# An expert stage that goes by experts in place of tiles of 128 tokens, with routing masks in bf16

## The reference, cut to what matters

```python
x = x + tanh(g_xattn[0]) * attention(layernorm(x), ctx, Wq, bq, Wk, bk, Wv, bv)   # B=8, S=256, H=256, 120 keys
h = layernorm(x)                                     # 2048 tokens of 256
logits = einsum('sbh,eh->sbe', h, router_w)          # E=8 experts
routing = argmax(logits, axis=-1)                    # one expert for each token
for e in range(8):
    mask = (routing == e)[..., None]
    xe = where(mask, h, 0.0)
    g = einsum('sbh,ih->sbi', xe, gate_w[e])         # I=704
    u = einsum('sbh,ih->sbi', xe, up_w[e])
    out = out + where(mask, einsum('sbi,hi->sbh', silu(g) * u, down_w[e]), 0.0)
x = x + tanh(g_ffn[0]) * out
```

## Time and profile before

| what | value |
|---|---|
| median of 3 runs | 226.1 us (225.43 to 228.0) |
| span of the profiled execution, first to last instruction | 218.9 us |
| median less span, what lies around the span | 7.2 us |
| TensorE, share of the span busy | 91% (199.7 us) |
| VectorE, ScalarE, GpSimd | 60%, 50%, 62% |
| granted TensorE clock, mean over the span | 0.960 |

### The profile page before, as it was taken

The page is one execution under the profiler, slowest core; times in us unless marked ns, Lnnn a source line. Parts: engine busy times, 40 slices in busy tenths (PEclk is TensorE's granted clock), DMA queues, the critical chain, the costliest instruction groups (busy, mean ns, idle before and its releaser), DMA issues.

```text
span 218.9 us, 4538 instructions
## 1 busy us (share of the span) xinstructions
PE 199.7 (91%) x1200; PEld 170.9 (78%) x1200; DVE 130.8 (60%) x430; ACT 109.8 (50%) x223; POOL 136.1 (62%) x138
## 2 busy tenths in 40 slices
PE   7899999997665789999999999999999999999960
PEld 3667998985564678888888888888888888888850
DVE  2886899867699125537555537564636565645650
ACT  1478777664500534495269485369475444422410
POOL 3004099495473897339966998987998985212111
PEclk9999999999787589999999999999999999999996
DMA  6999315928600319621581085194003012011000
GB/s 208 340 394 378 135 49 163 368 73 291 217 0 0 99 25 358 211 68 38 189 313 32 0 311 189 34 383 126 1 8 92 0 51 68 9 49 51 5 28 20
DMA packets 11845, 29.43 MB, mean 134 GB/s; under 512 B 1986, under 2 KB 8517, under 8 KB 10790
## 3 DMA queue, kind: packets, MB, share of 16 engines
q1 hardware_dynamic: 6320, 20.20, 25.9%
q0 software_dynamic: 2064, 5.12, 7.8%
q10 hardware_dynamic: 3430, 3.74, 5.1%
HBM read 24.85 MB, written 4.72 MB: 135 GB/s over the span
## 4 chain that ended last, share of the span: by engine, by line
PE 83%; DVE 6%; ACT 3%; DMA 3%; issue 2%; ACTq 1%; POOL 0%; POOLq 0%; DVEq 0%
PE ps L929 36%; PE ps L941 12%; PE ps L908 6%; PE ps L944 5%; PE ps L790 3%; PE ps L729 3%; PE ps L770 3%; DMA both<-in_ctxT 3%; PE ps L811 3%; PE ps L759 2%; PE ps L901 2%; PE ps L800 2%; PE ps L750 2%; PE ps L878 1%; DVE V L1193 1%
## 5 line engine op out<-in xcount | busy, mean ns | idle before, releaser
L929 PE MATMUL ps<-wgu,xhT 128*128 x360 | 83.1, 384 | 1.2 <-DVE xhT L1229 1.2
L929 PEld LDWEIGHTS ps<-wgu,xhT 128*128 128x128 f32 x360 | 66.3, 191 | 12.5 <-issue 1.6
L464 POOL DMA_INDIRECT xin<-x_rows,table x23 | 22.7, 986 | 29.4 <-DVE xin L1264 21.5
L941 PE MATMUL ps<-wd,hT 128*128 x114 | 40.5, 392 | 0.0
L396 POOL TENSOR_TENSOR wgu<-raw_gu,wgu (+1 forms) x12 | 38.6, 3253 | 0.1
L1246 DVE TENSOR_TENSOR A<-xin,ps 128x512 f32<-128x512 f32 (+1 forms) x40 | 20.6, 520 | 25.4 <-ACT xin L656 14.6
L656 ACT ACTIVATE xin<-ps 128x512 f32<-128x512 f32 (+1 forms) x40 | 18.6, 465 | 31.5 <-PE ps L929 31.1
L469 POOL DMA_INDIRECT out<-xin,table x20 | 20.3, 1015 | 18.3 <-DVE xin L1264 13.2
L650 ACT ACTIVATE hT<-ps 128x512 fp32r<-128x512 f32 x20 | 11.8, 592 | 32.9 <-PE ps L908 32.9
L944 PE MATMUL ps<-wd,hT 128*128 x95 | 26.6, 280 | 0.0
L941 PEld LDWEIGHTS ps<-wd,hT 128*128 128x128 f32 x114 | 21.3, 187 | 3.9
(11 more groups left out here) (163 smaller groups left out, 310.7 us busy)
## 6 DMA issues: line engine op xcount, KB each, us to landing
raw_gu<-in_Wgu SPq DMA_DIRECT2D x8, 1408.0 KB, 6.5
both<-in_Wd SPq DMA_DIRECT2D x8, 640.0 KB, 4.3
x_rows<-x ACTq DMA_DIRECT2D x8, 256.0 KB, 3.4
xin<-in_x SPq DMA_DIRECT2D x7, 256.0 KB, 8.8
both<-in_WdL SPq DMA_DIRECT2D x16, 64.0 KB, 4.7
both<-in_ctxT ACTq DMA_DIRECT2D x2, 480.0 KB, 7.1
xin<-x_rows,table POOLq DMA_INDIRECT x23, 3.6
out<-xin,table POOLq DMA_INDIRECT x20, 2.7
```

The source lines that it names most:

```text
L464: pool.indirect_dma_start(out=xg[:, j % SEATS, :], out_offset=None, in_=rows, in_offset=bass.IndirectOffsetOnAxis(ap=table[:, j:j + 1], ax ...
L929: last = pe.matmul(ps[:, g, 0:2 * WIDE if g < 2 else 4 * REST], xhT[:, j % 2, x_part, c, :], w, start=(c == 0 and (x_part, w_part) == (0, 0)),
L941: last = pe.matmul(ps[:, 6, 0:2 * H], hT[:, 0, c, :], wd[:, slot, c].rearrange("p o a n -> p (o a n)"), start=(c == 0), stop=(c == CI - 1) ...
```

## The change

The constants: `G = 336` tokens at most in a pass, in blocks of 128, 128 and 80 (`BLOCK`, `FULL = 2`), `SIZES = (256, 272, 336)`, `MORE` passes more for experts with over 336 tokens, and `SEATS = 5`, `AHEAD = 2`, `SHARE = 2`, `THIRD = 4`. There is one pass for each expert. In `up` the weights are now stationary and the tokens move: the pass has six chunks of 128 rows of h, the 64-row tail of gate and up together first (`ORDER`), with 6 matmuls for the tail and 12 for each of the five others, of 256, 272 or 336 columns by the expert's count. h comes out in the layout that `down` wants, so it is not transposed: VectorE multiplies in PSUM (`gated`), ScalarE copies the high part out of PSUM (`high_h`), VectorE subtracts (`low_h`). The widths on ScalarE and VectorE are 336 always.

```diff
+        def sized(eng, name, n_tokens, run):
...
+            with eng.If(n_tokens > SIZES[0]):
+                with eng.If(n_tokens > SIZES[1]):
+                    run(SIZES[2])
+                with eng.Else():
+                    run(SIZES[1])
+            with eng.Else():
+                run(SIZES[0])
...
@@ tensor @@
+            def product(j, i, kind, bank, n):
                 for c in range(C):
+                    for w_part, x_part in PASSES:
+                        last = pe.matmul(ps[:, bank, 0:n], weights(j, w_part, c, i, kind), xhT[:, j % 2, x_part, c, 0:n],
...
+            def up(j, s, n):
+                q = CI * j + s
+                i = chunk(q)
...
+                if q >= 2:
+                    pe.wait_ge(a_sg, q - 1)
+                if i < CI - 1:
+                    product(j, i, 0, gate_bank(q), n).then_inc(t_gu, 1)
+                    if q >= 3:
+                        pe.wait_ge(v_hT, q - 2)
+                    product(j, i, 1, up_bank(q), n).then_inc(t_gu, 1)
...
+            def down(j, n_tokens):
...
+                def add(k, s):
...
+                    pairs = [(2 * i, 0), (2 * i, 1), (2 * i + 1, 0)] if i < CI - 1 else [(2 * i, 0), (2 * i, 1)]
+                    for n, (h_part, w_part) in enumerate(pairs):
+                        last = pe.matmul(y_of(j, k), hT[:, h_part, some], wd[:, j % SPLIT, i, w_part, :],
...
+            for j in range(E):
+                for s in range(CI):
+                    sized(pe, "pe", sizes[j], lambda n: up(j, s, n))
...
+                if j + 1 < E:
+                    turn_x(j + 1, sizes[j + 1])
+                down(j, sizes[j])
...
             query_bias()
+            for _ in range(7):
+                pe.matmul(ps[:, 7, 0:2 * H], quiet[:, 0:P], quiet[:], start=True, stop=True)
             score_weights(0)
...
-            spin(64)
+            spin(52)
...
-            spin(24)
+            spin(34)
@@ scalar @@
+            split_first(B - 1)
+            act.wait_ge(v_slot, 1)
+            for t in range(THIRD):
+                act.activation(apart[:, t, :], iota_lo[:], ACT.Abs, scale=-1.0, bias=slot_f[:, t:t + 1]).then_inc(a_off, 1)
+            for t in range(THIRD):
+                act.wait_ge(a_off, t + 1)
+                ins = act.activation(ohlo[:, t, :], apart[:, t, :], ACT.Relu, scale=-1.0, bias=1.0)
+            ins.then_inc(a_lo, 1)
+            split_first(B)
...
+            for j in range(E):
+                chunks(j, 0, 2)
+                now = j and SPLIT <= j + AHEAD < E
+                if now:
+                    split_d(j + AHEAD, 0)
+                if j + 1 < E:
+                    gathered(j + 1, 0)
+                chunks(j, 2, 3)
+                if j + 1 < E:
+                    gathered(j + 1, 1)
+                chunks(j, 3, 4)
+                if j + 1 < E:
+                    gathered3(j + 1, sizes[j + 1])
+                if now:
+                    split_d(j + AHEAD, 1)
+                chunks(j, 4, CI)
+                if j + 1 < E:
+                    turned_x(j + 1)
+                high_h(CI * j + CI - 1)
...
+                if SPLIT <= j + SPLIT < E:
+                    split_gu(j + SPLIT)
@@ vector @@
-            link(dve.tensor_scalar(n_of, ps[:, 0, NTOK * E:(NTOK + 1) * E], 1.0, float(P - 1), ALU.max, ALU.add))
...
-            link(dve.tensor_tensor(offs, ends, padded, ALU.subtract))
+            link(dve.tensor_tensor(rk[:], ps[:, 0, 0:NTOK * E].rearrange("p (t e) -> p t e", e=E), oh[:, 0:NTOK, :], ALU.mult))
             link(dve.tensor_reduce(slot[:], rk[:], AX_X, ALU.add))
+            link(dve.tensor_tensor(slot_i[:, 0, :], slot[:], base[:], ALU.add))
...
+            for t in range(THIRD, NTOK - SHARE):
+                dve.tensor_scalar(ohlo[:, t, :], iota_lo[:], slot_f[:, t:t + 1], None, ALU.is_equal)
+            dims = [P, NT, NTOK]
+            link(dve.tensor_tensor(ohhi[:], iota_hi, slot_h[:].unsqueeze(1).to_broadcast(dims), ALU.is_equal))
...
+            dims = [P, 6, NT, NTOK]
+            dve.tensor_tensor(rsel[:], ohhi[:].unsqueeze(1).to_broadcast(dims),
+                              r3[:].rearrange("p a b t -> p (a b) t").unsqueeze(2).to_broadcast(dims),
+                              ALU.mult).then_inc(v_rsel, 1)
+            def experts(j, n_tokens, n_next):
+                for s in range(CI):
+                    gated(CI * j + s)
+                    if s:
+                        low_h(CI * j + s - 1)
...
@@ gpsimd @@
+            for j in range(AHEAD):
+                gather(j)
+            low_gu(SPLIT - 1, 1)
+            low_d(SPLIT - 1, 1)
+            for j in range(E):
+                if j + AHEAD < E:
+                    gather(j + AHEAD)
+                if SPLIT <= j + AHEAD < E:
+                    low_gu(j + AHEAD, 1)
+                    low_d(j + AHEAD, 1)
+                if j:
+                    scatter(j - 1)
+            scatter(E - 1)
```

More of the change, by code:

```diff
@@ new lines, in third, with gate_bank, up_bank @@
+        def third(eng, name, n_tokens, run, left_out=None):
+            if n_tokens is None:
+                run()
+                return
+            with eng.If(n_tokens > SIZES[0]):
+                run()
+                eng.sem_inc(idle, 1)
+            with eng.Else():
+                if left_out is not None:
+                    left_out()
+                eng.sem_inc(idle, 1)
+        def gate_bank(q):
+            return 2 * (q % 2)
+        def up_bank(q):
+            return (1, 3, 7)[q % 3]
@@ L489, in _, with fetch @@
[L489 to L503 removed]
+            def fetch(j, k, signal):
+                pool.indirect_dma_start(
+                    out=seat(j, k), out_offset=None, in_=rows,
+                    in_offset=bass.IndirectOffsetOnAxis(ap=index(j, k), axis=0)).then_inc(signal, 16)
@@ new lines, in gather @@
+            def gather(j):
+                r = j % SEATS
+                if j >= SEATS:
+                    third(pool, "pool", sizes[j - SEATS], lambda: pool.wait_ge(d_scat[r], 16 * BL),
+                          lambda: pool.wait_ge(d_scat[r], 16 * FULL))
+                for k in range(FULL):
+                    fetch(j, k, d_gath[r][k])
+                if j == 0:
+                    pool.wait_ge(v_used, 1)
+                sizes.append(count(pool, j))
+                third(pool, "pool", sizes[j], lambda: fetch(j, FULL, d_rest[r]))
@@ new lines, in chunks @@
+            def chunks(j, lo, hi):
+                for s in range(lo, hi):
+                    silu(CI * j + s)
+                    if s:
+                        high_h(CI * j + s - 1)
+            act.activation(negc[:, 0:1], negc[:, 0:1], ACT.Silu)
+            act.wait_ge(v_used, 1)
+            sizes = [count(act, 0)]
+            act.wait_ge(v_stat, 1)
+            for k in range(FULL):
+                gathered(0, k)
+            turned_x(0)
+            gathered3(0, sizes[0])
+            turned_x3(0, sizes[0])
@@ new lines, in run @@
+            def run(j):
+                if j == E:
+                    act.wait_ge(v_where, 2)
+                for k in range(FULL):
+                    gathered(j, k)
+                gathered3(j, None)
+                turned_x(j)
+                turned_x3(j, None)
+                split_gu(j)
+                split_d(j, 0)
+                split_d(j, 1)
+                chunks(j, 0, CI)
+                high_h(CI * j + CI - 1)
+                act.wait_ge(d_more_out, 16 * BL * (j - E + 1))
@@ L712, in _ @@
             pe.wait_ge(v_quiet, 1)
-            for _ in range(5):
-                pe.matmul(ps[:, 7, 0:2 * H], quiet[:, 0:P], quiet[:], start=True, stop=True)
+            for bank in (2, 3, 7, 7, 7):
+                pe.matmul(ps[:, bank, 0:2 * H], quiet[:, 0:P], quiet[:], start=True, stop=True)
             for c in range(C):
```

1020 lines of the change are left out of this document (553 added, 467 removed).

## The result

The changed kernel took **215.6 us** (median of five runs) against 226.1: a ratio of 0.956, 95% interval 0.949 to 0.962. So it is faster, but 12.6 us above the forecast of 203.0 and outside its range of 195 to 212. The profiled execution is one of its slower ones: 219.1 us, span 217.2.

A forecast was written before the change was run, and what follows sets the result against it. PE was taken as the bound, at 83% of the chain. The expert stage at -23.3 us and the start at +0.15 brought the span from 218.9 to 195.8; with 7.2 around it, 203.0 us, range 195 to 212.

The forecast's parts named there:

- `up`, `down` and transposes: PE's expert stage: matmul counts times prices gave 112.7 us, 114.4 with joints and slow start, against 137.7 before.
- A stage where nothing but PE is late is worth what its matmuls are worth: Expert stage: premise that counting and pricing PE's matmuls gives its time, then checking whether another engine takes over; -23.3 us.
- The start: Everything ahead of the expert stage: terms 0.95, 0.3, -1.5 and 0.4 us, together +0.15 us.
- To the sorting: Start up to VectorE's sorting chain: +0.95 us for seven added PE matmuls, +0.3 for ScalarE's splits in late attention.
- To the first gather: Sorting: fewer small VectorE operations and masks bring the table and first gather 2.7 us sooner.
- To the first `up`: First gather to first `up`: 7.0 us for 5.8, since the pass needs two gathers; +0.4 for a slow clock.
- 7.2 us around the span: Time outside the profiled span, taken as unchanged and added to the forecast span of 195.8 us.
- `rsel`: VectorE's wide sorting mask, 2304 elements: 2.6 us by the old rate; some 1.3 us by the skill's rule.
- GpSimd as the bound: Rival, expert stage: GpSimd's operations cost 15% more and expert 7's weights come 5 us late; 208 us, chance 0.12.
- ScalarE late within `up`: Rival: ScalarE's chain is late in each `up`, 1 us in passes with a split; +6, 209 us, chance 0.10.
- Jumps: Rivals, PE's 48 `up` chunks: 0.2 us a jump, 212.6 us, chance 0.05; waiting for code, 251 us, chance 0.04.
- Widths: Rival, `up`: the counts lead all passes to 336 columns; 225.7 us, no change, chance 0.03.

The follow-up runs named there:

- occasion I: First repeat of the changed kernel with no edit, on which no semaphore update was held: 202.7 us.
- the late split: Changed kernel with ScalarE's split of the third down weight moved from the seventh attention batch to behind the last: 197.3 us against 202.7.
- the quiet occasions: The repeats of the unedited changed kernel in which no semaphore update was held: 202.7, 202.4 and 203.3 us.
- III: A later repeat of the changed kernel with no edit, with no update held: 202.4 us.
- IV: The last repeat of the changed kernel with no edit, with no update held: 203.3 us.
- the one attempt in the kernel before: Kernel before the change, with gathers and scatters of three tiles issued together, six in a row: 240.1 us against 224.0, with no held update.

## Why the prediction was wrong, step by step

- **The sign and the mechanism held.** `up`, `down` and transposes: 112.7 us plus joints and a slow start, 114.4, measured 111.9, 110.5 and 111.9 where nothing is held. Undoing the widths costs 15.0 for 14.
- **The step that failed** is "A stage where nothing but PE is late is worth what its matmuls are worth". I looked for other engines that are late, found GpSimd's sum of work, and took its order for harmless ("most gathers have somewhere to go"). The change turns GpSimd's pairs and fours into runs of up to six, and on some occasions PE's semaphore updates are held while such runs are issued; the stage is then 128.1 us for the forecast 114.4. No rival had this. It is worth 12 us (214.9 against 202.7 and 202.4), of which spreading the runs gives 9 back. In the profiled execution of the first measurement, 219.1 us, the sum misses by 16.1: the stage was forecast 13.7 too low, the start 7.7 too low (82.85 for 75.00 against +0.15) and what lies outside the span 5.4 too high. The kernel before issues up to four in a row and has no held update in its trace.
- **The start was forecast at +0.15 us; it is +7.0** on occasion I: the first `up` at 81.98 for 75.00. *To the sorting*, forecast +1.25: VectorE's chain there starts at 64.35 for 59.27, +5.1, of which the first score product is 1.3 (9.90 for 8.59). I saw that the split "needs `wd` of expert 2" and priced the wait, not what PE's gap behind it does to the clock; the late split takes 3.5 us off here, beside the same occasion's trace. *To the first gather*, forecast -2.7: 7.3 us (64.35 to 71.66) for 9.9, so -2.6. *To the first `up`*, forecast +1.2 and +0.4: 10.3 us for 5.8, +4.5. I priced the PE side of the new layout at nothing, and its 16 products take 4.3 us where 1.9 stood; at a granted clock of 0.55 the 34 spins behind them are on the path (76.19 to 79.76, 0.105 us each).
- **7.2 us around the span** was the runs' median less one execution's span. The outside is 1.8 us after (202.19 against 200.4) and 2.1 before (224.49 against 222.4); the profiled execution of before was a quick one.
- So 203.0 agrees with the 202.4 to 203.3 of the quiet occasions by luck, by cancelling: on I the span is forecast 4.6 us too low (the start 6.9 too low, the stage 2.5 too high, 0.2 at the end), the outside 5.4 too high.
- **`rsel`.** It took 1.35 us for 2304 bf16 elements, where 1104 took 1.30 before. The Trainium skill, page "VectorE: DVE Perf Modes", section "What auto-detection actually checks", had it right and my 2.6 us had not.
- **The strided operand** has a rule too that I did not weigh: the Trainium skill, page "SBUF — State Buffer", section "Door 1: The DMA port swizzle (why `[64,N]` ≈ `[32,N]`)", says that reads which leave a 16-byte line each time pay a penalty. With a step of 32 bytes a product of 48 columns took 0.099 us, contiguous 0.036, both at full granted clock; the trace agrees.
- **The rivals.** GpSimd as the bound, ScalarE late within `up`: on the quiet occasions I, III and IV PE has no gap of over 0.15 us behind the first product of `up`. Jumps: 0.01 us a pass. Widths: the passes are of 256, 272 and 336 as counted.

What stays open: what it is that the occasion adds, and which part of an indirect transfer goes with the holds. A rival is untested: the recording of the trace. In the seven traces that have held updates 29 to 57 of some 850 update records are missing, in all the others at most 6, and every time here has a recorded span and clock beside it, so no run shows whether updates are held without a recording. I tried neither fewer bytes in a gather nor the same run without loads beside it; the one attempt in the kernel before fell on a quiet occasion.

## What to carry to other kernels

Put GpSimd's gathers and scatters between its other work, one or two at a time, even where it has time to spare: it cost nothing when nothing was held and gave back 9 of 12 us when updates were; what was left stood mostly behind the one run of six that remained. Time a close result on more than one occasion, and when two engines start in the same hundredth of a microsecond long after the work that they wait for, look at the semaphore events and not at the engines; but believe a late record only where the waiting engine is late too. Where a transpose of a mask's layout makes VectorE quicker, price the matmul that reads it, and keep PE busy through a short wait ahead of a long stage.

## What was not expected of the hardware

- PE's semaphore updates arriving up to 4.2 us late, several released within 0.25 us, while GpSimd issues indirect transfers in a row; 20 and 25 of 88 on two occasions, none on three others with the same program. No update of ScalarE's or VectorE's is recorded late with its waiter late too.
- A bf16 moving operand with a step of 32 bytes costs 2.1 ns a column at full granted clock (1.58 us/16/48), contiguous 0.75 (0.58/16/48). Over 144 columns it is 1.9 ns (4.32 us/16/144, clock 0.62 or 0.56) against 0.6 (0.67/8/144, clock 1.00).
- A gap of 1.6 us in PE's work was followed by some 13 us at a granted clock of 0.50, in a stretch where PE is busy for 5 us in 6 or 7. It does not come out the same each time: on III, behind a gap of 1.4 us, the clock is 0.86 from 54 to 60 us and 0.63 from 60 to 67. The windows of the first measurement:

```profile
51.00:54.00 3.00, 1.37 (x8) 1.04 (x8) 2.48 (x15) 1.76 (x2) 3.00 (x4) 0.87 0.27 97
54.00:60.00 6.00, 5.06 (x20) 3.88 (x18) 2.00 (x10) 0.82 (x2) 1.96 (x4) 0.50 0.58 186
60.00:67.00 7.00, 5.22 (x48) 5.13 (x49) 3.87 (x25) 2.23 (x4) 4.63 (x20) 0.51 0.24 87
```
